# One step of each quantisation of tokens as a ScalarE Relu, the roundings as operations of three operands, and a new order of the work

## The reference

```python
_GRID = [0.0, 0.5, 1.0, 1.5, 2.0, 3.0, 4.0, 6.0]
_MID = [0.25, 0.75, 1.25, 1.75, 2.5, 3.5, 5.0]
def fp4_quant_dequant(x):                      # blocks of 16 along the last dim
    scale = max(max(abs(xb)) / 6, 1e-12)
    xn = xb / scale
    q = _GRID[searchsorted(_MID, abs(xn))] * sign(xn) * scale
def fp4_linear(x, w):
    return einsum('bsk,nk->bsn', fp4_quant_dequant(x), fp4_quant_dequant(w))
h = silu(fp4_linear(x, w_gate)) * fp4_linear(x, w_up)     # 352 wide
y = fp4_linear(h, w_down)
x = layernorm(x + y)
```

## Time and profile before

| what | value |
|---|---|
| median of 3 runs | 747.43 us (747.34 to 751.6) |
| the profiled execution's own time | 747.63 us |
| its span in the trace | 745.8 us |
| granted PE clock, mean | 0.848 of full speed |
| busy: PE, DVE, ACT, POOL | 557.3, 532.0, 326.2, 203.9 us |

### The profile page before, as it was taken

How to read it: one execution, slowest core, us unless ns; L and a number is a source line. 1 busy time by engine, 2 the same in 40 slices (tenths; PEclk the granted TensorE clock), 3 DMA queues, 4 the chain that set the end, 5 groups by cost and what they waited for, 6 DMA issues and landing times.

```text
span 745.8 us, 13887 instructions
## 1 busy us (share of the span) xinstructions
PE 557.3 (75%) x4864; PEld 389.2 (52%) x4864; DVE 532.0 (71%) x1520; ACT 326.2 (44%) x637; POOL 203.9 (27%) x316
## 2 busy tenths in 40 slices
PE   5697668666488869687885696566888797789954
PEld 3466536434255337454674364354453375687841
DVE  7877777898758667657776678987676676765734
ACT  1653345322275556115633462222864551354631
POOL 4304300201100620274024011021016112774533
PEclk9997669888789989769977697976999795699987
DMA  9993100000000000020000000000000000332324
GB/s 293 324 296 108 29 0 2 1 1 0 2 0 1 1 1 2 1 80 14 2 2 0 1 2 1 0 2 0 1 1 0 1 3 1 89 115 71 84 88 115
DMA packets 45555, 32.34 MB, mean 43 GB/s; under 512 B 4280, under 2 KB 43456, under 8 KB 45360
## 3 DMA queue, kind: packets, MB, share of 16 engines
q1 hardware_dynamic: 43216, 26.54, 12.8%
q0 software_dynamic: 2272, 4.92, 1.9%
HBM read 13.83 MB, written 17.62 MB: 42 GB/s over the span
## 4 chain that ended last, share of the span: by engine, by line
PE 46%; DVE 33%; ACT 9%; issue 6%; POOL 2%; DMA 2%; DVEq 0%; SPq 0%; POOLq 0%; ACTq 0%
PE ps L624 5%; PE ps L605 5%; PE ps L668 5%; PE ps L943 5%; PE ps L957 2%; DVE s_row_max L1344 2%; DVE s_probs L1349 2%; ACT s_probs L1084 2%; PE ps L874 2%; PE ps L869 2%; DVE s_r L1313 2%; PE ps L636 2%; DVE s_work L1303 1%; DVE s_work L1300 1%; DVE s_work L1290 1%
## 5 line engine op out<-in xcount | busy, mean ns | idle before, releaser
L1883 POOL TENSOR_TENSOR s_rs<-s_mv,eps 128x1 f32<-128x1 f32 x80 | 16.4, 207 | 347.0 <-DVE s_mv L1319 346.9
L1344 DVE TENSOR_REDUCE s_row_max<-ps 128x16 f32<-128x1024 f32 x48 | 58.7, 1222 | 41.6 <-PE ps L624 41.4
L605 PE MATMUL ps<-tabs,s_probs 128*128 128x128 f32 x384 | 63.2, 295 | 17.1 <-ACT s_probs L1084 15.8
L1064 ACT ACTIVATE s_pT<-ps 128x512 f32<-128x512 f32 x96 | 55.6, 594 | 39.0 <-PE ps L605 38.5
L624 PE MATMUL ps<-s_k,s_q 64*64 64x256 f32 x768 | 61.0, 442 | 9.9 <-ACT s_q L1034 9.9
L605 PEld LDWEIGHTS ps<-tabs,s_probs 128*128 128x128 f32 x384 | 44.2, 148 | 37.7 <-ACT s_probs L1084 25.7
L1084 ACT ACTIVATE s_probs<-s_probs 128x1024 f32<-128x1024 f32 x48 | 50.6, 1056 | 24.5 <-DVE s_probs L1349 24.5
L1349 DVE TENSOR_TENSOR s_probs<-ps,s_row_max 128x1024 f32<-128x1024 f32 x48 | 58.7, 1222 | 1.3
L668 PE MATMUL ps<-s_v,s_pT 128*64 128x18 f32 x1536 | 56.2, 218 | 4.1 <-ACT s_headsT L1075 1.9
L668 PEld LDWEIGHTS ps<-s_v,s_pT 128*64 128x64 f32 x1536 | 52.4, 146 | 11.8 <-issue 11.0
L943 PE MATMUL ps<-s_pT,s_k 128*128 128x128 f32 x312 | 44.5, 287 | 4.6 <-issue 2.8
(11 more groups left out here) (285 smaller groups left out, 1262.9 us busy)
## 6 DMA issues: line engine op xcount, KB each, us to landing
rows_io<-zero_rows SPq DMA_DIRECT2D x9, 1152.0 KB, 11.9
s_probs<-rows_io SPq DMA_DIRECT2D x39, 72.0 KB, 1.9
s_cin<-in_ctx SPq DMA_DIRECT2D x4, 256.0 KB, 3.7
s_xin<-in_x SPq DMA_DIRECT2D x4, 256.0 KB, 4.3
wgu<-in_wg SPq DMA_DIRECT2D x1, 1024.0 KB
wgu<-in_wu SPq DMA_DIRECT2D x1, 1024.0 KB
wo<-in_wo SPq DMA_DIRECT2D x1, 1024.0 KB
s_probs<-shares_io SPq DMA_DIRECT2D x4, 256.0 KB, 5.2
```

The costliest lines, as they stand in the source:

```text
L605: ins = pe.transpose(h.ps[:, 2, tile(j)], h.probs[:, t % 2, 8 * part + 2 * j:8 * part + 2 * j + 2, :] .rearrange("p h k -> p (h k)"), ident)
L1064: act.activation(h.pT[:, t % 2, 4 * part:4 * part + 4, :].rearrange("p j q -> p (j q)"), h.ps[:, 2, :], ACT.Copy).then_inc(h.pT_here.sem, 1)
L1344: dve.tensor_reduce(h.row_max[:, t % 2, :], s3, AX, ALU.max).then_inc(h.max_here.sem, 1)
```

## The change

Five edits.

1. On DVE, line 1297 is gone from each quantisation of tokens. In its place ACT computes Relu(MAGIC * e - MAGIC) in place, on 256 columns for a half of x and on 352 for a hidden tile (`round_by`, line 1123 in the changed kernel). DVE's v + e waits for it. max(e, 1) * MAGIC is that Relu plus MAGIC.
2. The MAGIC that is then missing is added in the next two DVE operations, which take three operands now: (e + MAGIC) + v, and (e + MAGIC) - v. The second has the other sign, so the last operation multiplies by -1 as well. The weights' quantisations keep the old form.
3. POOL sets a new constant `minus_magic` of one column, first of its set-ups.
4. The Relus stand in ACT's program as steps of their own: the first half's at the tail of the cross-attention, the second half's ahead of the taking of `xT`, tile u's after that tile's Silu and the tile before's copy.
5. All four tables of `ORDER` are new numbers; the steps keep their sequence within each stream.

```diff
-        0, 1, 0, 3, 2, 0, 1, 1, 0, 1, 1, 0, 1, 1, 0, 3, 3, 0, 3, 1, 0, 1, 1, 0, 2, 1, 0, 1, 1, 0, 2, 1, 0,
...
+        1, 1, 0, 2, 2, 0, 1, 1, 0, 1, 1, 0, 1, 1, 0, 3, 3, 0, 3, 1, 0, 1, 1, 0, 2, 2, 0, 3, 1, 0, 2, 1, 0,
...
+        minus_magic = sb("minus_magic", [P, 1])
...
-                yield from attention_tiles(h, 1)
+                yield from attention_tiles(h, 1, None, {2: lambda h: round_by(h, 0, TOK // 2)})
...
+            def round_by(h, n, columns):
+
+                yield
+                act.wait_ge(set_up, SET_UP["minus_magic"])
+                act.wait_ge(*h.fq.at(8 * n + 5))
+                act.activation(h.qe[:, 0:columns], h.qe[:, 0:columns], ACT.Relu, scale=MAGIC, bias=minus_magic[:, :]).then_inc(h.fq.sem, 1)
+
             def ffn(h):
                 if h is streams[0] and h.turn == 0:
                     take_fp4_weights(h)
+                yield from round_by(h, 1, TOK // 2)
...
+                    if u < TILES:
+                        yield from round_by(h, 2 + u, FFN)
...
-                dve.wait_ge(*sig.at(count + 5))
-                dve.tensor_scalar(e, e, 1.0, MAGIC, ALU.max, ALU.mult).then_inc(sig.sem, 1)
-                yield
+                if sig is once:
+                    dve.wait_ge(*sig.at(count + 5))
+                    dve.tensor_scalar(e, e, 1.0, MAGIC, ALU.max, ALU.mult).then_inc(sig.sem, 1)
+                    yield
+                    dve.wait_ge(*sig.at(count + 6))
+                    dve.tensor_tensor(v, v, e, ALU.add).then_inc(sig.sem, 1)
+                    yield
+                    dve.wait_ge(*sig.at(count + 7))
+                    dve.tensor_tensor(v, v, e, ALU.subtract).then_inc(sig.sem, 1)
+                    yield
+                    dve.wait_ge(*sig.at(count + 8))
+                    return dve.tensor_tensor(dst, v3, over(m), ALU.mult)
+
+
                 dve.wait_ge(*sig.at(count + 6))
-                dve.tensor_tensor(v, v, e, ALU.add).then_inc(sig.sem, 1)
+                dve.scalar_tensor_tensor(v, e, MAGIC, v, ALU.add, ALU.add).then_inc(sig.sem, 1)
                 yield
                 dve.wait_ge(*sig.at(count + 7))
-                dve.tensor_tensor(v, v, e, ALU.subtract).then_inc(sig.sem, 1)
+                dve.scalar_tensor_tensor(v, e, MAGIC, v, ALU.add, ALU.subtract).then_inc(sig.sem, 1)
                 yield
                 dve.wait_ge(*sig.at(count + 8))
-                return dve.tensor_tensor(dst, v3, over(m), ALU.mult)
+                return dve.scalar_tensor_tensor(dst, v3, -1.0, over(m), ALU.mult, ALU.mult)
...
+            pool.memset(minus_magic[:, :], -MAGIC).then_inc(set_up, 1)
```

More of the change, by code:

```diff
@@ L108 @@
 BLOCK_POOL = steps("n_eps 1", "n_rstd 1", "n_eps 2", "n_rstd 2")
-SET_UP = steps("minus_half", "eps", "zero_rows", "v_zeros 1", "v_zeros 2", "ones 1", "ones 2", "ones 3", "ones 4",
+SET_UP = steps("minus_magic", "minus_half", "eps", "zero_rows", "v_zeros 1", "v_zeros 2", "ones 1", "ones 2", "ones 3", "ones 4",
                "zeros 1", "zeros 2", "conv_mids")
```

## The result

The changed kernel takes **768.56 us** (median of 4 runs, 764.32 to 769.63) where the kernel before, measured beside it, takes 749.48: ratio 1.0244, 95% interval 1.0188 to 1.0300. It is slower, outside the range. A second measurement on another chip gave 1.0222 (1.0175 to 1.0270). The profiled execution took 768.01 us with a span of 766.2, against 747.63 and 745.8.

The account below looks back on a forecast made before the run. DVE, 87% busy, was taken to bound the feed-forward stage; 747.63 us + 0.4 (waits against removal) + 0.8 (ACT's queue) + 0.5 (weights) + 0.4 (`xt_here`) = 749.7, less 0.2 for the median: 749.5 us, range 741.5 to 756.

Parts of the forecast that it names:

- The swaps of neighbours in the other stages: Outside the feed-forward stage, reordered neighbours keep each stream's chain and cost nothing, with 3 us either way.
- The removal: -7.9 us: Taking the step off DVE in 24 quantisations of tokens, priced by starts in the timeline, gives -7.9 us.
- 9.5 us of waiting, 87% counted: 8.3: DVE's waits for the Relus, 87% counted as DVE idles 13% of the feed-forward stage; +0.4 us net of the removal.
- ACT's queue: Relu of stream 1's half starts late behind other ACT work, once per turn: 2 x 0.4 = +0.8 us (0 to 1.5).
- weights: At the taking of weights, a Relu stands ahead of three ACT copies and stream 1's probabilities: +0.5 us (0 to 1.1).
- `xt_here`: At DVE's wait for `xt_here`, the whole 2.37 us shows where DVE idled 1.92 before: +0.4 us (0 to 0.45).
- At nothing: Three-operand DVE operations and the new constant's set-up cost nothing, 0.3 us if not free; swaps in other stages also nothing.
- The rival "chain": The chain through one quantisation decides, so no cover counts: 4.9 us in place of 0.4, 754.0 us; chance 0.15.
- What would show me wrong: Idle ahead of DVE's 1321 under 5 us, feed-forward windows shorter by over 2 us, or time moving in attention stages.

Follow-up runs that it names:

- e11: Kernel before with VectorE's new order everywhere but in the two feed-forward stages (189 positions differ), against the kernel before: 1.0066 (1.0037 to 1.0096), 5 us.
- e10: Kernel before with VectorE's steps in the new order in the two feed-forward stages alone, against the kernel before: 1.0177 (1.0146 to 1.0208), 13 us.
- e7: Kernel before with only GpSimd's order table new, against the kernel before: 1.0002 (0.9979 to 1.0025).

## Why the prediction was wrong

- **"The swaps of neighbours in the other stages I also put at nothing, with 3 us either way."** This step failed. The new order costs 10.7 us (1.0143), nearly all of it by VectorE's table. Outside the feed-forward stages that table costs 5 us by itself (e11, 2.8 to 7.2), where 3 were allowed. The swaps in these stages stood in no term at all, only as cover for gaps, and cost 13 us (e10). They kept each stream's chain, as I said; what they broke was the alternation of two chains. That shows in 2.8 us of busy time; how the 6.9 us of idling come from it stays open.
- **"The removal: -7.9 us."** Measured -3.5. The starts were read rightly, step by step, but the sum treats each as if DVE were always what ends last. Of 7.6 us, 1.3 never left DVE's busy time, and 2 to 3 became waits for other engines. The 13% of idle time was put on the waits and not on the gain.
- **"9.5 us of waiting, 87% counted: 8.3."** The waits were 12.1 in the changed kernel and 10.8 in the old order, mis-sized by 1 to 3 us. The factor was wrong too, as far as the intervals tell: 10.8 us of waits cost 10 to 11, all of them and not 87%. The term, forecast at +0.4 with +2.4 as its upper bound, is 6.6 to 7.4 together with the next two points.
- **ACT's queue, weights, `xt_here`.** At the named places the profile shows 1.10 in place of 0.64, and 2.51 in place of 1.92. They were right in kind; what they cost, 1.7 us in the forecast, was not measured by itself.
- **At nothing.** Right for the operations of three operands: they take 523 ns for 352 columns, as 1290 did, and 424 for 256.
- **The rival "chain"**, 4.9 us in place of 0.4, is nearest to what the arithmetic did: no cover counts, 4.9 + 1.7 = 6.6. That the number fits is in part luck: it sets 16 x 0.63 + 8 x 0.56 = 14.6 us of gaps against 16 x 0.42 + 8 x 0.37 = 9.7 of removed steps, where the runs gave 10 to 11 against 3.5. The rule of the Trainium skill tied to it, relu on VectorE, holds here (1.0088 with the Relu on ScalarE). I gave the rival 0.15, because two streams interleave. Interleaving left 10.8 us of waits, and these cost about their length.
- **What would show me wrong** was partly the wrong list. The idle time was above 5 us and the windows did not get shorter, so neither sign spoke against the forecast. "If the time moves in the attention stages" came true only in part, with 2.7 us in the causal one. I didn't list that the feed-forward windows get longer. DVE's busy time fell by 2.9 and not by 7.6 as the list had it, which is the sign of the lost overlap.

Left open: which of the 122 swapped positions cost. One group of 22 in the first turn gives 0.15% of the 1.77; the rest was not taken apart. How much of the order's cost goes through TensorE's clock is also open: raising it brought nothing in the kernel before and 0.5%, not certain, in the changed one. What makes up the 5 us outside the feed-forward stages (e11) is open too.

## What to carry to other kernels

Where two streams share an engine, price an edit from a chain in both directions: here removed work gave half its length and added waits cost about all of theirs, and a round trip to another engine must be shorter than the step that it replaces (from the mask's end to the sum 0.71 us against 0.42 here) or wholly covered. An order table that comes with an edit is a change of its own: measure it without the edit first. When one profile says that a clock or a stage explains the loss, ask the medians of an experiment that mends just that.

## What the runs showed of the hardware

- Neighbours on VectorE overlap by 0.08 to 0.09 us when the second doesn't depend on the first, and stand 0.03 to 0.04 apart when it does; with 390 instructions in these stages this came to 2.8 us of busy time for the same instructions in another order.
- Behind a stop of 1.11 us TensorE stayed at 1.2 GHz, through 2.71 us of matmuls that took 1.45 at 2.4 GHz where the stop was filled.
- A Relu in place in SBUF, with a scale and a bias operand, takes ScalarE 586 ns for 352 columns and 507 for 256; VectorE idles 0.71 and 0.64 us for one that nothing covers.
- Filling 16 waits with 64 matmuls cost nothing measurable (1.0019) and raised the granted clock only in parts.
- Chips differ: the kernel before takes 750 us on some and 770 to 773 on others. The feed-forward stages are alike on both (140.4 and 141.2 us in e7 and e11); from the end of the second one to the end of the execution it is 228 us against 247.
